# Replanning the takes of a graph-attention, mixing and FP4 feed-forward layer, with seven base chunks ahead of its tail

## The chip, the cores and the metric

One core of a Trainium2 chip runs the whole layer as one program with five instruction streams: TensorE (PE), VectorE (DVE), ScalarE (ACT), GpSimd (POOL) and SyncE (SP). The metric is the time of one execution on the device in microseconds, the median of several.

## The reference

`x` is 1250 x 1024 in float32, with 40000 edges `src -> dst`, sorted by `dst`.

```python
xn = layernorm(x)
x = x + gnn(xn, src, dst) + mix(xn)
x = x + ffn(layernorm(x))

gnn: h = rms_norm(xn) * rms_w @ W_down            # 1024 -> 256
     xl, xr = h @ Wl, h @ Wr                      # 4 heads of 64
     e = sum(leaky_relu(xl[src] + xr[dst]) * att) # per edge and head, self loops added
     out = softmax over the edges of each dst, weighting xl[src];  out @ W_up
mix: q, k, v = xn @ W.T + b;  (q @ k.T * SCALE) @ v @ Wo.T + bo   # no softmax
ffn: gate, up = fp4(y) @ fp4(gate_w).T, fp4(y) @ fp4(up_w).T
     fp4(silu(gate) * up) @ fp4(down_w).T         # blocks of 16 with e4m3 scales
```

## The kernel before, in words

The 1250 rows are ten chunks of 128 (the last has 98). Since the mixing has no softmax, it is computed as a chain of 1024 x 1024 products: the Gram matrix of the normalized rows, then `p`, `kv`, `t1`, `t2` (16 groups each, a group being one 128 x 512 result of eight accumulated products), at whose end one matrix stands in `big_a`; `base` is `xhat` times that matrix, two groups for each chunk, plus bias and x.

**Start.** SP loads x chunk by chunk (L442), between chunks 1 and 2 also the RMS weights as a column (L445) and `w_down` (L446). VectorE normalizes (L1308 to L1316), TensorE transposes (`turn_rows`, L805), ScalarE scales `w_down` by the RMS weights (`scale_wd`, L1106).

**Rounds.** The edges of the graph are worked in 62 rounds of up to six neighbours for each of 128 nodes. In each, POOL gathers rows (L564) and rescales (L686), VectorE forms scores (L1532, L1701, L1703, L1708) and sums (L1540), ScalarE takes exponentials (L1167) and multiplies (L1177). Meanwhile TensorE works through the groups `p` to `base` (L782) in four PSUM banks of `acc`: group n may begin once group n-4 has been taken. A take is one instruction, on VectorE for `p`, `kv`, `p0c` and `bias` (L1492, L1495, L1489, L1500), on ScalarE for `t1`, `t2` and `base` (L1090, L1096, L1093). Both engines run a fixed order, so a small planner (the loop that fills `round_of`, constants `PRODUCTS_AT`, `ROUND_0_AT`, `GROUP_STEP`, `SLOT_STEP`, `ROUND_OVER`, `TAKE_STEP`) gives every take the round at whose begin it stands. A take too late holds TensorE up, one too early the engine that takes.

**Tail.** The first `EARLY` chunks have their base before the tail. x is added to these by an accumulating transfer of POOL (`add_x`, L699), the bias too (`add_bias`, L708). For the later chunks SP loads x (L533) and the base products are made in the tail, inside `x2` (L939), with the two products of the graph part (L942). `X2_PLAN` gives for each (chunk, half) the bank, when TensorE makes it and when VectorE adds it to the residual (L1658). In iteration k of the tail TensorE transposes the quantized chunk k+1 (`turn_q`, L961), then the hidden chunk k-2 (L983), makes its x2, the down product of k-2 (L996) and gate and up of k+1 (`gate_up`, L972), which are sixteen products with one signal at their end. ScalarE normalizes chunk k+2 (L1058, L1059), copies the transposes (L1208, L1235), computes `silu` (L1243) and scales the down product (L1200), in this fixed order. VectorE's step k finds block maxima (L1300), scales and rounds chunk k+1 together with hidden chunk k-1 (L1632 to L1646), after the product silu * up (L1612).

Of the kernel before, what the change touches and what calls it, by code (L numbers as in the profile page):

```python
# [9 lines left out]
F32 = mybir.dt.float32  # L10
# [18 lines left out]
EARLY = 6  # L29
# [29 lines left out]
PRODUCTS_AT, GROUP_STEP = 168, {"p0c": 2.0, "bias": 1.0}  # L59
ROUND_0_AT, SLOT_STEP, ROUND_OVER, TAKE_STEP = 158, 0.95, 2.2, 0.7  # L60
# [3 lines left out]
BIAS_SUMS_AT, AHEAD = 43, 2  # L64
# [55 lines left out]
def gps_layer(nc, x, src, dst, rms_w, w_down, wl, wr, att, w_up, wq, bq, wk_t, bk, wv_t, bv,  # L120
# [9 lines left out]
    with ExitStack() as ctx:  # L130
# [72 lines left out]
        rms_col = sb("rms_col", [P, KB])  # L203
        s_in_bc = sb("s_in_bc", [P, 2])
# [26 lines left out]
        wd_in, rms_in, wlr_in = sem("wd_in"), sem("rms_in"), sem("wlr_in")  # L231
        edges_in = sem("edges_in")
# [56 lines left out]
        gu_full, silu_done, hid_done = sem("gu_full"), sem("silu_done"), sem("hid_done")  # L289
# [89 lines left out]
        off_ps = tpb[0:DG_HI, 1, 2 * DG_LO:2 * DG_LO + 2].bitcast(F32)  # L379
        lin_ps = tpb[0:NC, 0, 0:4 * H * C].bitcast(F32).rearrange("p (c h) -> p c h", c=C)  # L380
# [56 lines left out]
        def _(sp):  # L437
            for c in range(C):
# [4 lines left out]
                if c == 1:  # L443
                    with nc.allow_non_contiguous_dma(reason="columns of small vectors"):
                        sp.dma_start(rms_col[:], rms_w.rearrange("(k p) -> p k", p=P)).then_inc(rms_in, 16)  # L445
                    sp.dma_start(wd_sb, w_down.rearrange("(k p) d -> p k d", p=P)).then_inc(wd_in, 16)  # L446
# [317 lines left out]
        def _(pe):  # L764
# [46 lines left out]
            for c in range(2):  # L811
                turn_rows(c)
# [151 lines left out]
            def gate_up(c):  # L964
# [9 lines left out]
                mm.then_inc(gu_full, 1)  # L974
# [29 lines left out]
            for k in range(-1, C + 2):  # L1004
# [6 lines left out]
                if k == 2:  # L1011
                    turn_hidden(0)
                if 0 <= k - 2 < C:
                    down(k - 2)
                if 0 <= k + 1 < C:
# [8 lines left out]
        for g, (_, _, slots, _, _) in enumerate(ROUNDS):  # L1024
            while n < len(groups):
                kind, i, engine = groups[n]
                full = max(at, freed.get(n - 4, 0)) + GROUP_STEP.get(kind, 7.0)
                if full > begun:
# [3 lines left out]
                freed[n] = begun + 0.8  # L1032
# [12 lines left out]
        def _(act):  # L1045
# [63 lines left out]
            act.wait_ge(rms_in, 16)  # L1109
            act.wait_ge(wd_in, 16)  # L1110
            for k in range(3):
                scale_wd(k)
            take_rows(1)
            for k in range(3, KB):
# [110 lines left out]
            for k in range(-1, C + 2):  # L1225
# [13 lines left out]
                if 0 <= c < C:  # L1239
                    act.wait_ge(gu_full, c + 1)  # L1240
# [7 lines left out]
        def _(dve):  # L1248
# [353 lines left out]
            def tail_scales(k):  # L1602
# [6 lines left out]
                if k - 1 >= 0:  # L1609
                    c = k - 1  # L1610
                    dve.wait_ge(silu_done, c + 1)
# [153 lines left out]
```

## Time and profile before

| | us |
|---|---|
| median of 3 executions | 902.01 (901.41 to 905.28) |
| the profiled execution, own time | 905.27 |
| its span, first to last instruction | 903.4 |
| TensorE busy / VectorE busy | 855.8 / 794.7 |
| ScalarE busy / POOL busy | 563.1 / 497.2 |

The profiled execution's time is 1.9 us longer than its span. Matmul records are pipelined, and a 128x512 product in float32 has two records. The granted clock is TensorE's, as a share of 2.4 GHz, 0.50 being 1.2 GHz.

### The profile page before, as it was taken

The numbers are of one execution on the slowest core, as the hardware profiler recorded it, in microseconds if no ns is written. First come the engines' busy times: TensorE is split into PE (matmuls) and PEld (weight loads), VectorE is DVE, ScalarE is ACT, GpSimd is POOL, SyncE is SP. The second block draws the span as 40 slices with busy tenths as digits, with TensorE's granted clock in tenths as the row PEclk, the third lists the DMA queues.
The fourth block names the chain that finished last, engine by engine and source line by source line (L and its number), as shares of the span: only waits on it lengthen the run. The fifth ranks groups of instructions, "written<-read, shape, count | busy, mean of one in ns | idle before, by whom it ended". The sixth has DMA issues, their size and how long they took to land.

```text
span 903.4 us, 9499 instructions
## 1 busy us (share of the span) xinstructions
PE 855.8 (95%) x2744; PEld 421.2 (47%) x2754; DVE 794.7 (88%) x903; ACT 563.1 (62%) x1977; POOL 497.2 (55%) x527
## 2 busy tenths in 40 slices
PE   6899999999999999999999999999699999999855
PEld 5786455644444444444444444444244444444322
DVE  6999989689999999999999999999993078788994
ACT  3317532387658778779898988789894243243432
POOL 3405588667667677777777878877751130010001
PEclk7989999999999999999999999999699999999878
DMA  9331773735354433554336634338936563222335
GB/s 300 112 124 25 230 200 102 246 89 88 73 177 148 122 88 102 192 186 120 100 99 195 195 97 103 90 92 193 265 84 134 116 155 93 79 43 46 47 47 88
DMA packets 66578, 114.83 MB, mean 127 GB/s; under 512 B 29575, under 2 KB 36516, under 8 KB 66506
## 3 DMA queue, kind: packets, MB, share of 16 engines
q0 software_dynamic: 22144, 63.68, 30.2%
q1 hardware_dynamic: 44378, 50.51, 17.4%
q8 instruction: 22, 0.36, 0.2%
q14 instruction: 34, 0.28, 0.1%
HBM read 89.28 MB, written 17.17 MB: 118 GB/s over the span
## 4 chain that ended last, share of the span: by engine, by line
DVE 59%; PE 32%; issue 4%; ACT 3%; DMA 1%; SPq 0%; ACTq 0%; POOL 0%; DVEq 0%
PE acc L782 21%; DVE acc_sb L1540 11%; DVE z L1703 10%; DVE turned L1532 10%; DVE turned L1701 10%; PE acc L939 2%; PE acc L972 2%; PE turned L939 2%; PE acc L942 2%; PE turned L996 1%; ACT round_mem L1177 1%; DVE z L1708 1%; DVE big_b L1492 1%; DMA big_b<-in_x 1%; DVE big_a L1495 1%
## 5 line engine op out<-in xcount | busy, mean ns | idle before, releaser
L564 POOL DMA_INDIRECT round_mem<-msg_table,idx x352 | 349.5, 993 | 103.0 <-issue 82.6
L1177 ACT ACTIVATE round_mem<-round_mem,pz 128x65 f32<-128x65 f32 x1408 | 354.0, 398 | 6.8 <-DVE acc_sb L1540 2.8
L782 PE MATMUL acc<-wslot,big_a 128*128 128x512 f32 x512 | 220.3, 593 | 0.0
L782 PEld LDWEIGHTS acc<-wslot,big_a 128*128 128x128 f32 x512 | 97.3, 190 | 121.3 <-issue 121.1
L1540 DVE TENSOR_REDUCE acc_sb<-round_mem 128x260 f32<-128x1820 f32 (+1 forms) x62 | 121.6, 1962 | 14.1 <-ACT round_mem L1177 12.0
L782 PE MATMUL acc<-big_b,wslot 128*128 128x512 f32 x256 | 110.0, 593 | 0.0
L782 PE MATMUL acc<-wslot,big_b 128*128 128x512 f32 x256 | 110.0, 593 | 0.0
L1532 DVE TENSOR_TENSOR turned<-round_mem,turned 128x1560 f32<-128x1560 f32 (+1 forms) x62 | 105.4, 1700 | 2.3 <-DMA round_mem<-msg_table,idx 0.2
L1703 DVE TENSOR_REDUCE z<-turned 128x24 f32<-128x1560 f32 (+1 forms) x62 | 105.1, 1696 | 2.1
L1167 ACT ACTIVATE pz<-z 128x7 f32<-128x7 f32 (+1 forms) x248 | 55.4, 295 | 78.9 <-DVE z L1708 77.9
L1701 DVE SCALAR_TENSOR_TENSOR turned<-turned,att_sb 128x1536 f32<-128x1536 f32 (+1 forms) x62 | 103.6, 1671 | 0.1
L782 PE MATMUL acc<-big_a,xhat_t 128*128 128x512 f32 x192 | 85.6, 609 | 6.0 <-ACT big_b L1093 6.0
L782 PE MATMUL acc<-big_b 128*128 128x512 f32 (+3 forms) x240 | 78.7, 487 | 0.0
L782 PEld LDWEIGHTS acc<-big_b,wslot 128*128 128x128 f32 x256 | 48.7, 190 | 61.1 <-issue 60.6
L782 PEld LDWEIGHTS acc<-wslot,big_b 128*128 128x128 f32 x256 | 48.7, 190 | 61.1 <-issue 61.1
L782 PEld LDWEIGHTS acc<-big_a,xhat_t 128*128 128x128 f32 x192 | 37.5, 196 | 54.6 <-issue 46.6
L686 POOL TENSOR_TENSOR round_mem<-acc_sb,pz 128x260 f32<-128x260 f32 x62 | 44.1, 711 | 33.1 <-DVE acc_sb L1540 28.1
L782 PEld LDWEIGHTS acc<-big_b 128*128 128x128 f32 x240 | 42.3, 191 | 34.0 <-issue 28.4
L1243 ACT ACTIVATE round_mem<-acc,cscale 128x512 f32<-128x512 f32 x10 | 6.9, 687 | 73.8 <-PE acc L972 61.7
L735 POOL TENSOR_TENSOR rstd<-small,minus_half 128x1 f32<-128x1 f32 x10 | 6.3, 626 | 81.8 <-ACT small L1190 81.8
L741 POOL DMA_DIRECT2D out_x<-acc_sb x9 | 7.9, 878 | 74.8 <-ACT acc_sb L1200 74.8
L782 PE MATMUL acc<-xhat_t,big_a 128*128 128x256 f32 x160 | 40.6, 414 | 3.1 <-ACT xhat_t L1101 3.1
(231 smaller groups left out, 1009.8 us busy)
## 6 DMA issues: line engine op xcount, KB each, us to landing
big_b<-in_x SPq DMA_DIRECT2D x12, 512.0 KB, 9.8
round_mem<-msg_table,idx POOLq DMA_INDIRECT x352, 2.8
big_b<-big_b POOLq DMA_DIRECT2D x9, 512.0 KB, 5.9
out_x<-big_b SPq DMA_DIRECT2D x9, 512.0 KB, 3.1
out_x<-acc_sb POOLq DMA_DIRECT2D x9, 512.0 KB, 5.6
wslot<-in_wv_t SPq DMA_DIRECT2D x2, 2048.0 KB, 9.9
wslot<-in_wk_t SPq DMA_DIRECT2D x2, 2048.0 KB, 9.4
wslot<-in_wo_t SPq DMA_DIRECT2D x2, 2048.0 KB, 9.6
```

Source lines behind the costliest of these rows:

```text
L564: pool.indirect_dma_start(xg[g % 4][:, j, :], None, msg_table, bass.IndirectOffsetOnAxis(idx[:, c, j0 + j:j0 + j + 1], 0)).then_inc(xg_in[ ...
L686: nc.gpsimd.tensor_tensor(halves_of[g % 3][:, :, :, n].rearrange("p i (h d) -> p i h d", d=MR), running[c].rearrange("p (i h d) -> p i h d ...
L782: mm = nc.tensor.matmul(o(acc[:, n % 4, :]), a, b, start=first, stop=last)
L939: nc.tensor.matmul(to, xhat_t[:, k, c * NC:(c + 1) * NC], mat_a[:, k, h * HALF:(h + 1) * HALF], start=(k == 0), stop=False)
L942: mm = nc.tensor.matmul(to, gnn_tr[:, k, c * NC:(c + 1) * NC], wup_sb[:, k, h * HALF:(h + 1) * HALF], start=(c < EARLY and k == 0), stop=( ...
L972: mm = nc.tensor.matmul(acc[0:NC, 2 + h, :], q_t[c % 2][:, k, 0:NC], wgu_sb[:, k, h * HALF:(h + 1) * HALF], start=(k == 0), stop=(k == KB ...
L1167: ins = nc.scalar.activation(pz[:, g % 2, 0:slots + 1, h], z[:, g % 3, 0:slots + 1, h], ACT.Exp, scale=-1.0, bias=z[:, (g + 1) % 3, top_sl ...
L1177: ins = nc.scalar.activation(to[:, :, j], xg[g % 4][:, j, h * HR + 1:(h + 1) * HR], ACT.Copy, scale=pz[:, g % 2, j, h:h + 1])
L1532: return nc.vector.tensor_tensor(m4[:, 0:n], xg[g % 4][:, 0:n, :].rearrange("p j (h d) -> p j h d", d=HR)[:, :, :, 0:MR], receiver.unsquee ...
L1540: nc.vector.tensor_reduce(running[c].rearrange("p (i f) -> p i f", i=2), halves_of[g % 3][:, :, :, 0:n + 1], AX.X, ALU.add).then_inc(sum_d ...
L1701: step(nc.vector.scalar_tensor_tensor(m4[:, 0:slots, :, 1:MR], m4[:, 0:slots, :, 1:MR], 0.0, att_sb[0:NC].unsqueeze(1).to_broadcast([NC, s ...
L1703: step(nc.vector.tensor_reduce(zz[:, 0:slots, :], m4[:, 0:slots], AX.X, ALU.add))
```

## The change

Four edits in one:

1. The planner's constants and rules are replaced, so most takes move one or two rounds up. The sums for the bias start a round earlier (`BIAS_SUMS_AT` 43 to 42).
2. `EARLY` is 7: chunk 6's two base groups come before the tail. In `X2_PLAN` (7, 1) takes the place and bank of (6, 1).
3. The RMS weights are loaded as eight rows of 128, transposed by TensorE and copied to the column by ScalarE.
4. `gate_up` signals after the gate half too; silu waits for this alone and VectorE for both. For the last chunk gate and up are put ahead of a down product.

```diff
-EARLY = 6
+EARLY = 7
-PRODUCTS_AT, GROUP_STEP = 168, {"p0c": 2.0, "bias": 1.0}
-ROUND_0_AT, SLOT_STEP, ROUND_OVER, TAKE_STEP = 158, 0.95, 2.2, 0.7
+PRODUCTS_AT, GROUP_STEP = 173.5, {"p0c": 2.0, "bias": 1.0}
+ROUND_0_AT, SLOT_STEP, ROUND_OVER, TAKE_STEP = 166.5, 0.95, 2.2, 0.7
...
-BIAS_SUMS_AT, AHEAD = 43, 2
+BIAS_SUMS_AT, AHEAD = 42, 2
...
-    (5, 1, 2, (-2, 7), (0, 0)), (2, 1, 0, (-2, 7), (-1, 2)), (6, 1, 6, (-2, 7), (0, 2)), (2, 0, 5, (-2, 9), (-1, 2)),
+    (5, 1, 2, (-2, 7), (0, 0)), (2, 1, 0, (-2, 7), (-1, 2)), (7, 1, 6, (-2, 7), (0, 2)), (2, 0, 5, (-2, 9), (-1, 2)),
...
-    (7, 1, 4, (0, 0), (3, 0)), (6, 0, 1, (0, 1), (2, 0)), (7, 0, 6, (1, 0), (3, 0)), (5, 0, 0, (1, 0), (2, 2)),
+    (6, 1, 4, (0, 0), (2, 0)), (6, 0, 1, (0, 1), (2, 0)), (7, 0, 6, (1, 0), (3, 0)), (5, 0, 0, (1, 0), (2, 2)),
...
-                    with nc.allow_non_contiguous_dma(reason="columns of small vectors"):
-                        sp.dma_start(rms_col[:], rms_w.rearrange("(k p) -> p k", p=P)).then_inc(rms_in, 16)
+                    sp.dma_start(rms_rows[:], rms_w.rearrange("(k p) -> k p", p=P)).then_inc(rms_in, 16)
...
-            for c in range(2):
-                turn_rows(c)
+            turn_rows(0)
+            pe.wait_ge(rms_in, 16)
+            nc.tensor.transpose(rms_ps, rms_rows[:], ident[0:KB, 0:KB]).then_inc(rms_tp, 1)
+            turn_rows(1)
...
-                mm.then_inc(gu_full, 1)
+                    mm.then_inc(gate_full if h == 0 else gu_full, 1)
...
+                if k + 1 == C - 1:
+                    gate_up(k + 1)
                 if 0 <= k - 2 < C:
                     down(k - 2)
-                if 0 <= k + 1 < C:
+                if 0 <= k + 1 < C - 1:
                     gate_up(k + 1)
...
-                full = max(at, freed.get(n - 4, 0)) + GROUP_STEP.get(kind, 7.0)
-                if full > begun:
+                full = max(at, freed.get(n - 4, 0)) + GROUP_STEP.get(kind, 6.93)
+                if full > begun + (2.5 if engine == "act" else 0.0):
                     break
                 round_of[n], at = g, full
                 begun += TAKE_STEP if engine == "dve" else 0.0
-                freed[n] = begun + 0.8
+                freed[n] = begun + (0.8 if engine == "dve" else 3.6)
...
             take_rows(0)
-            act.wait_ge(rms_in, 16)
+            act.wait_ge(rms_tp, 1)
+            nc.scalar.copy(rms_col[:], rms_ps).then_inc(rms_taken, 1)
+            act.wait_ge(rms_taken, 1)
             act.wait_ge(wd_in, 16)
-            for k in range(3):
+            for k in range(2):
                 scale_wd(k)
             take_rows(1)
-            for k in range(3, KB):
+            for k in range(2, KB):
                 scale_wd(k)
...
-                    act.wait_ge(gu_full, c + 1)
+                    act.wait_ge(gate_full, c + 1)
...
                     dve.wait_ge(silu_done, c + 1)
+                    dve.wait_ge(gu_full, c + 1)
```

The order on ScalarE at the end of the rounds, before (an `ACTIVATE big_a<-acc` is a take of `t2`, a `COPY big_b<-acc` one of `base`, `pz<-z` and `round_mem<-round_mem,pz` the exponentials and multiplications of a round):

```order
L1096 ACTIVATE big_a<-acc 128x512
L1167 ACTIVATE pz<-z 128x7 x4
L1177 ACTIVATE round_mem<-round_mem,pz 128x65 x24
L1096 ACTIVATE big_a<-acc 128x512
L1167 ACTIVATE pz<-z 128x6 x4
L1177 ACTIVATE round_mem<-round_mem,pz 128x65 x20
L1096 ACTIVATE big_a<-acc 128x512
L1167 ACTIVATE pz<-z 128x7 x4
L1177 ACTIVATE round_mem<-round_mem,pz 128x65 x24
L1093 COPY big_b<-acc 128x512
```

and after, over the same rounds:

```order
L1102 ACTIVATE big_a<-acc 128x512
L1175 ACTIVATE pz<-z 128x7 x4
L1185 ACTIVATE round_mem<-round_mem,pz 128x65 x24
L1099 COPY big_b<-acc 128x512
L1175 ACTIVATE pz<-z 128x6 x4
L1185 ACTIVATE round_mem<-round_mem,pz 128x65 x20
L1099 COPY big_b<-acc 128x512
L1175 ACTIVATE pz<-z 128x7 x4
L1185 ACTIVATE round_mem<-round_mem,pz 128x65 x24
L1099 COPY big_b<-acc 128x512
```

These are rounds 53, 54, 55 and the begin of 56. Where the last three takes of `t2` stood, now the last of `t2` and the first two of `base` stand, and the third of `base` has the first one's place.

The order on TensorE in iteration 0 of the tail, before (`L961` the transposes of chunk 1, `L939` base products, `L942` those of the graph part, `L972` gate and up):

```order
L961 MATMUL turned<-identb,round_mem 128x128 x8
L939 MATMUL turned<-big_a,xhat_t 128x512 x8
L942 MATMUL turned<-wslot,xr_sb 128x512 x2
L972 MATMUL acc<-wslot,round_mem 128x512 x16
L939 MATMUL acc<-big_a,xhat_t 128x512 x8
L942 MATMUL acc<-wslot,xr_sb 128x512 x2
L961 MATMUL turned<-identb,round_mem 128x128 x8
```

and after:

```order
L965 MATMUL turned<-identb,round_mem 128x128 x8
L946 MATMUL turned<-wslot,xr_sb 128x512 x2
L976 MATMUL acc<-wslot,round_mem 128x512 x16
L946 MATMUL acc<-wslot,xr_sb 128x512 x2
L965 MATMUL turned<-identb,round_mem 128x128 x8
```

The sixteen base products between the two transposes are gone; those of (7, 1) stand where (6, 1) stood, and chunk 6's stand ahead of the tail.

On POOL, in the tail's first iterations, the change (`L701` and `L737` are `add_x` and the root of the deviation, `L710` is `add_bias`):

```order
L737 TENSOR_TENSOR rstd<-small,minus_half 128x1
L701 DMA big_b<-in_x 128x1024
L710 DMA big_b<-big_b 128x1024 x3
L737 TENSOR_TENSOR rstd<-small,minus_half 128x1 x2
L701 DMA big_b<-in_x 98x1024
```

The first transfer of x (chunk 6) is new here; the three biases behind it are those of chunks 4, 8 and 6, before 4, 8 and 7.

## Rows read from the trace of the kernel before

**Rows 1.** The page: busy time of the engines, and the chain's shares.

```profile
PE 855.8 (95%) x2744; PEld 421.2 (47%) x2754; DVE 794.7 (88%) x903; ACT 563.1 (62%) x1977; POOL 497.2 (55%) x527
...
DVE 59%; PE 32%; issue 4%; ACT 3%; DMA 1%; SPq 0%; ACTq 0%; POOL 0%; DVEq 0%
```

**Rows 2.** Timeline of PE: start, us, engine, line, instruction, idle before.

```profile
175.40 15.19 PE L782 MATMUL acc<-wslot,big_a 128*128 128x512 f32 x35
...
630.39 1.02 PE L782 MATMUL acc<-big_b,minus_half 128*128 128x512 f32 x2
634.62 2.06 PE L782 MATMUL acc<-big_b,minus_half 128*128 128x512 f32 x2 [3.22 <-ACT big_a L1096]
642.70 19.77 PE L782 MATMUL acc<-big_a,xhat_t 128*128 128x512 f32 x39 [6.01 <-ACT big_b L1093]
```

**Rows 3.** Timeline of ACT, takes.

```profile
618.91 0.58 ACT L1096 ACTIVATE big_a<-acc 128x512 f32<-128x512 f32 x1
...
641.97 0.58 ACT L1093 COPY big_b<-acc 128x512 f32<-128x512 f32 x1
...
714.43 0.58 ACT L1093 COPY big_b<-acc 128x512 f32<-128x512 f32 x1 [6.28 <-PE acc L782]
```

**Rows 4.** Busy time by stretch: length, PE, PEld, DVE, ACT, POOL, clock, DMA.

```profile
642.70:648.57 5.87, 5.87 (x8) 2.49 (x9) 5.65 (x6) 5.57 (x23) 4.54 (x6) 0.52 1.03 394
851.67:859.45 7.78, 7.69 (x23) 2.82 (x24) 7.33 (x14) 1.88 (x6) 0.56 (x1) 0.69 0.24 46
```

**Rows 5.** Timeline of DVE, begin of round 2.

```profile
185.74 1.76 DVE L1701 SCALAR_TENSOR_TENSOR turned<-turned,att_sb 128x1536 f32<-128x1536 f32 x1
```

**Rows 6.** Timeline of DVE, statistics of the third chunk.

```profile
13.43 0.69 DVE L1313 BATCH_NORM_STATS2 stats<-big_b 128x6 f32<-128x512 f32 x1 [3.91 <-DMA big_b<-in_x]
```

**Rows 7.** Transfers of 0 to 16 us: GB/s by 0.4 us, one issue's landing.

```profile
GB/s 0 0 0 0 113 174 317 389 440 348 430 358 61 76 50 206 315 305 330 289 266 302 371 425 405 443 394 443 399 420 430 399 440 410 420 420 420 420 399 420
...
rms_col<-in_rms_w SPq DMA_DIRECT2D x1, 4.0 KB, 7.4
```

**Rows 8.** Chain of waits, where TensorE takes over: start, us.

```profile
45.14 2.85 PE turned L790 x80
```

**Rows 9.** Busy time by TensorE iteration of the tail (columns as rows 4).

```profile
749.80:771.74 21.94, 21.29 (x64) 9.63 (x65) 15.88 (x30) 5.16 (x9) 0.56 (x1) 1.00 0.21 66
771.74:785.99 14.25, 14.20 (x48) 6.52 (x48) 13.43 (x22) 2.94 (x6) 1.49 (x2) 1.00 0.18 28
785.99:801.33 15.34, 14.61 (x56) 6.78 (x57) 14.72 (x27) 7.45 (x15) 1.73 (x2) 1.00 0.26 103
...
832.15:848.16 16.01, 14.81 (x56) 6.73 (x57) 13.53 (x23) 7.51 (x13) 1.43 (x2) 1.00 0.23 34
```

**Rows 10.** Timeline of DVE in the tail; L1300 begins a step.

```profile
764.66 1.03 DVE L1646 TENSOR_TENSOR round_mem<-round_mem 128x1024 bf16<-128x1024 bf16 x2
...
771.94 0.69 DVE L1658 SCALAR_TENSOR_TENSOR big_b<-acc,big_b 128x512 f32<-128x512 f32 x1 [5.64 <-PE acc L942]
...
773.34 1.75 DVE L1300 TENSOR_REDUCE round_mem<-round_mem 128x96 f32<-128x1536 f32 x1
...
804.78 1.75 DVE L1300 TENSOR_REDUCE round_mem<-round_mem 128x96 f32<-128x1536 f32 x1 [1.78 <-ACT round_mem L1059]
...
850.33 1.75 DVE L1300 TENSOR_REDUCE round_mem<-round_mem 128x96 f32<-128x1536 f32 x1 [0.62 <-ACT round_mem L1059]
...
863.87 1.75 DVE L1300 TENSOR_REDUCE round_mem<-round_mem 128x96 f32<-128x1536 f32 x1
```

**Rows 11.** The page: group of silu.

```profile
L1243 ACT ACTIVATE round_mem<-acc,cscale 128x512 f32<-128x512 f32 x10 | 6.9, 687 | 73.8 <-PE acc L972 61.7
```

**Rows 12.** Timelines of PE, ACT, DVE around the last silu.

```profile
879.02 3.19 PE L996 MATMUL turned<-wslot,round_mem 128*128 128x512 bf16 x7 [1.68 <-ACT round_mem L1235]
...
887.16 1.11 ACT L1200 ACTIVATE acc_sb<-turned,cscale 128x1024 f32<-128x1024 f32 x1
...
887.29 0.75 DVE L1612 SCALAR_TENSOR_TENSOR round_mem<-acc,cscale,round_mem 128x512 f32<-128x512 f32 x1 [3.35 <-ACT round_mem L1243]
```

More of the change, by code:

```diff
@@ L203, in gps_layer @@
         rms_col = sb("rms_col", [P, KB])
+        rms_rows = sb("rms_rows", [KB, P])
         s_in_bc = sb("s_in_bc", [P, 2])
@@ L231, in gps_layer @@
         wd_in, rms_in, wlr_in = sem("wd_in"), sem("rms_in"), sem("wlr_in")
+        rms_tp, rms_taken = sem("rms_tp"), sem("rms_taken")
         edges_in = sem("edges_in")
@@ L288, in gps_layer @@
         q_done, q_tp, q_taken = sem("q_done"), sem("q_tp"), sem("q_taken")
-        gu_full, silu_done, hid_done = sem("gu_full"), sem("silu_done"), sem("hid_done")
+        gate_full, gu_full, silu_done, hid_done = sem("gate_full"), sem("gu_full"), sem("silu_done"), sem("hid_done")
         h_done, h_tp, h_taken = sem("h_done"), sem("h_tp"), sem("h_taken")
@@ L379, in gps_layer @@
         off_ps = tpb[0:DG_HI, 1, 2 * DG_LO:2 * DG_LO + 2].bitcast(F32)
+        rms_ps = tpb[:, 0, 0:2 * KB].bitcast(F32)
         lin_ps = tpb[0:NC, 0, 0:4 * H * C].bitcast(F32).rearrange("p (c h) -> p c h", c=C)
```

## The prediction

> **What bounds the kernel now.** I read the page first: TensorE is busy for 95% of the span and VectorE for 88%, yet the chain that ended last runs 59% through VectorE and 32% through TensorE [rows 1]. Two engines are full side by side, so I went to the timeline of each and asked at every stretch which one the other waits for.
>
> Three facts come out of it.
>
> First, TensorE works without a gap from 175.40 us, where the "p" products begin, up to 630.39 [rows 2]. That is 66 groups (16 each of p, kv, t1 and t2, two of base) and one tiny one, so a group of eight 128x512 products takes (630.39 - 175.40) / 66 = 6.89 us. Then it stands still twice: 3.22 us before the second bias product, until ScalarE has taken t2's last group, and 6.01 us before the third base group, until ScalarE has taken the first base group at 641.97 [rows 2, 3]. These groups were full long before (t2's last at 175.4 + 64 x 6.89 + 0.5 = 616.9, the first base group at 623.8). They waited for their place in the table of takes, and a bank is refilled only when the take four groups back is done. After the second stall the granted clock is 0.52, the lower of the two levels (1.2 of 2.4 GHz), for 5.87 us in which eight matmul records run instead of some fourteen: 2.9 us more lost [rows 4]. VectorE's rounds end long before TensorE's last base group (taken at 714.43 [rows 3]) and the tail cannot start earlier. So TensorE's stream sets the time from the start of the products to the start of the tail.
>
> Second, ahead of that: VectorE stands 3.91 us until the third chunk of x lands at 13.4 [rows 6], from there works through, and hands to TensorE at 45.14 [rows 8], from where the chain is TensorE's. What chunk 2 gains, all gains.
>
> Third, the tail. Each TensorE iteration begins with the transposes of a quantized chunk. From 785.99 to 848.16 four of them take 15.5 us each and hold 14.6 to 14.8 us of TensorE work [rows 9]: nearly TensorE's pace, plus a wait. VectorE's own step is 13.5 us (850.33 to 863.87 [rows 10]). After 850 VectorE sets the pace.
>
> **The change, part by part.**
>
> *Takes replanned.* I moved every take to its new round and set full times at 6.89 us a group against the rounds' begins. The first p group, full at 182.3, is taken at the begin of round 2, at 185.7 with its own 0.7 us added [rows 5]: no wait. At the end t2's last group (full 616.9) takes ScalarE's slot at 618.91, and each base group a slot two places earlier than now; the slot of 641.97, which held the first base group, holds the third (full 639.7) [rows 3]. No group is taken before it is full, and no bank is asked for before its take. Both stalls go, and with them the clock's fall: 3.22 + 6.01 + 2.9 = **-12.1 us**. What is late next is TensorE itself.
>
> *Seven chunks ahead.* Two more base groups, 2 x 6.89 = **+13.8 us** before the tail.
>
> *RMS weights as rows.* The column load is 4 KB, 7.4 us to landing. While its 4-byte pieces run, four slices of 0.4 us carry 61, 76, 50 and 206 GB/s where the slices around reach 350 to 440 [rows 7]: 1.6 us that do 0.4 us of work, so 1.2 us lost ahead of w_down and chunk 2. Eight rows of 512 B cost next to nothing of that. The bounds are 0 (chunk 2 late for another reason) and 3.91, all of VectorE's wait; I take the slices' value, **-1.2 us**. The added transpose and the small copy lie before ScalarE's wait for w_down and are hidden by it; without that cover they would cost two small operations, under 0.5 us. By the Trainium skill, DMA: Bandwidth & Descriptors, section "Measured (HBM→SBUF, 128 partitions, SWDGE, issued from GpSimd)", a packet costs about 10.5 ns and 64 of them on an engine 0.67 us; as an estimate the term would be -0.7 and the sum half a microsecond worse.
>
> Start of the tail: 13.8 - 12.1 - 1.2 = **+0.5 us**.
>
> *The tail without chunk 6.* TensorE's iteration 0 (749.80 to 771.74) is 21.3 us of work, 13.8 of it the base products of two halves: (7, 1), which moves up into the place of (6, 1), and (6, 0), whose base is now done before the tail; both are gone from here [rows 9]. VectorE waits 5.64 us for just these, before 771.94 [rows 10]. In the new order VectorE has both residuals of chunk 6 at once, so its step 2 starts at 766.3 + 2 x 0.6 + 0.8 = 768.3 in place of 773.34. TensorE is done with iteration 0 at 771.74 - 13.8 = 757.9 and has nothing until the next chunk is quantized at 765.4 (the first half of the pair at 764.66 [rows 10]): **a new gap of some 7.5 us**. After the stall of 6.01 us and after a gap of 2.7 us before 851.67 the clock stood at 0.52 and 0.69 [rows 4]; so I expect it to fall here, for 2.8 us of lost work. Iteration 1 then runs 765.4 + 14.2 + 2.8 = 782.4 (before 785.99). The Trainium skill, TensorE: Matmul & The Clock Gate, section "What's actually happening", says the lower rate is the default and only activity lifts it, so idling is paid again on return; that speaks against this edit and agrees with rows 4. Were it not so here, the first rival below holds.
>
> *silu on the gate product alone.* Silu and the normalization queued behind it on ScalarE start one half, 1.7 us, earlier. That is the 1.78 us VectorE waits for the normalization before 804.78 [rows 10], in two steps of four, and smaller ones. So iterations close up to TensorE's own work: 15.3 for iteration 2 (its wait for the first hidden transposes stays), then 14.7 three times: 782.4, 797.7, 812.4, 827.1, 841.8, before 848.16. VectorE's step 7 begins 1.8 us after gate and scale are through, at 843.6, before 850.33: **-6.7 us**. From there both kernels run at 13.5 us a step.
>
> *Last gate and up ahead of a down product.* The last silu now waits for nothing but the gate. VectorE's wait of 3.35 us at 887.29 shrinks to 0.7, but that is not the end's chain: ScalarE's scaling of down product 6, which follows silu (0.69 us [rows 11]) at 887.16 [rows 12], starts the alternation of down, scale, copy that ends the kernel. It moves only to the end of the down product, some 886.1, as the same TensorE work lies ahead of it: **-1.0 us** (bounds 0, and -3.8 if the half clock of 879.02 [rows 12] and its 2.8 us weren't met).
>
> *Chunk 6's x* is now added by a POOL transfer put ahead of the bias of chunk 4, for which VectorE doesn't wait now. Bounds 0 and +1.2, half a megabyte at the 420 GB/s of rows 7; I take 0, since no wait for a bias shows in the tail.
>
> **Sum:** +0.5 - 6.7 - 1.0 = **-7.2 us**. The profiled execution's own time is 905.27 (span 903.4), which would become 898.1. It is 3.3 us above the median 902.01; on the median the same step gives **894.8 us**.
>
> **Rivals.**
>
> *The clock holds in the new gap.* For it: it was 1.00 across iteration 0 [rows 9], with short gaps only. Against: rows 4. Then iteration 2 starts when VectorE's step 2 delivers, 768.3 + 12.45 = 780.75 (a step's first result comes 12.45 us after its begin, as from 773.34 to 785.8), and all later ones 1.6 us earlier: 893.2. Chance 0.15.
>
> *The stalls were dearer in this execution than in the median one.* The 3.3 us between them are about one fall of the clock. If the median execution had the stalls but not the fall, 2.9 us of my gain aren't there: 897.7. Chance 0.2.
>
> *The plan misses, and TensorE still stalls (slower).* If ScalarE, whose multiplications fill most of each round, comes to the moved takes after its multiplications and thus as late as now, the 12.1 us stay while 13.8 us were added: 902.01 + 4.9 = 906.9. It decides from 7.2 us of remaining stall on; below that the tail still pays. Against it: the new slots are ScalarE's own take slots of now, filled one group further on. Chance 0.06.
>
> *The RMS edit does nothing* (chunk 2 lands as before): 896.0. Within the range; part of the forecast's 0.59.
>
> **How the numbers follow.** Likeliest 894.8, chance 0.59. Range: below, the clock holding (893.2) with 2 us more of chunk 2's wait, 891.2; above, the second rival with the RMS term at nothing, 898.9. This leaves out the slower case and a little of each end. A measurement here can tell 0.5%, 4.5 us, so the border is 897.5: faster 0.80 (0.55 of the forecast's 0.59, the first rival, half of the second), same 0.16 (the rest of both and the slower case where it falls just inside), slower 0.04.
>
> **What would show it.** TensorE's products without a wait from about 174 until about 715, clock 1.00 throughout; the third chunk's statistics near 12.2; a TensorE gap of 7 to 8 us near 758 with a lower clock behind it; no VectorE wait for the normalization in steps 3 to 7; iterations of 14.7 us. A stall of several microseconds among the base groups, or VectorE waiting for a product at a take, would prove the plan wrong; a tail that keeps 15.5 us per iteration would prove the silu term wrong.

## The result, and the profile after

| | before | changed |
|---|---|---|
| median, this comparison | 903.49 us (901.41 to 905.28, 4 runs) | 894.26 us (893.55 to 895.54, 4 runs) |
| ratio, 95% interval | | 0.990 (0.987 to 0.993) |
| median, a later comparison | 904.07 us (11 runs) | 894.04 us (4 runs), ratio 0.989 (0.987 to 0.990) |
| profiled execution, own time; span | 905.27; 903.4 | 895.54; 893.7 |
| TensorE busy / VectorE busy | 855.8 / 794.7 | 853.9 / 794.1 |

The kernel is 9 to 10 us faster, and my 894.8 lies 0.5 to 0.8 us from the measured medians. How much of that is merit is the question of the last sections, since the step itself was forecast at -7.2 us and measured at -9.2 to -10.0.

The page of the changed kernel, the chain's shares (before: [rows 1]):

```profile
PE 853.9 (96%) x2755; PEld 422.0 (47%) x2755; DVE 794.1 (89%) x903; ACT 564.4 (63%) x1980; POOL 495.6 (55%) x528
...
PE 84%; DVE 7%; issue 5%; DMA 2%; ACT 1%; POOL 0%; SPq 0%; ACTq 0%; DVEq 0%; POOLq 0%
```

TensorE has 84% of the chain, after 32%. It is not busier. Before, the chain left TensorE at the second stall and went back through VectorE's rounds to their begin; now there is no stall through which it could leave.

TensorE's timeline around the place of the stalls (start, us, engine, line, instruction, idle before), to be held against [rows 2]:

```profile
603.44 11.32 PE L784 MATMUL acc<-big_b,wslot 128*128 128x512 f32 x26
614.60 13.90 PE L784 MATMUL acc<-big_a,xhat_t 128*128 128x512 f32 x32
628.33 1.88 PE L784 MATMUL acc<-big_b,minus_half 128*128 128x512 f32 x4
630.04 82.14 PE L784 MATMUL acc<-big_a,xhat_t 128*128 128x512 f32 x191
```

No idle time stands behind any row: from 604 to 712 TensorE is busy for all 108.0 us at clock 1.00. The twelve remaining base groups take 82.4 us, 6.87 each, and the tail's first transposes start at 712.45. Before, they started at 714.23, with two groups fewer ahead of them.

ScalarE's last take of `t2` and its first three of base groups (compare [rows 3]) show by how much they moved:

```profile
616.03 0.58 ACT L1102 ACTIVATE big_a<-acc 128x512 f32<-128x512 f32 x1
...
625.26 0.58 ACT L1099 COPY big_b<-acc 128x512 f32<-128x512 f32 x1
...
631.47 0.58 ACT L1099 COPY big_b<-acc 128x512 f32<-128x512 f32 x1
...
639.44 0.58 ACT L1099 COPY big_b<-acc 128x512 f32<-128x512 f32 x1
```

The first base group was taken at 641.97 and is now taken at 625.26.

The tail, TensorE's iterations (length, then busy time of PE, PEld, DVE, ACT, POOL, clock, DMA; before: [rows 9]):

```profile
748.02:763.62 15.60, 7.93 (x33) 3.38 (x33) 14.98 (x28) 5.16 (x9) 0.56 (x1) 0.85 0.40 96
763.62:780.53 16.91, 16.91 (x48) 7.81 (x49) 16.29 (x31) 4.44 (x9) 1.49 (x2) 0.84 0.23 56
780.53:795.87 15.34, 14.66 (x57) 6.79 (x56) 12.99 (x22) 7.26 (x15) 1.18 (x2) 1.00 0.26 103
795.87:810.36 14.49, 14.49 (x57) 6.71 (x56) 12.71 (x20) 6.65 (x12) 1.57 (x2) 1.00 0.24 38
825.15:839.88 14.73, 14.70 (x58) 6.83 (x57) 13.89 (x24) 6.44 (x12) 1.43 (x2) 1.00 0.24 37
```

Read the first two together. Iteration 0 shrank from 21.94 to 15.60 us but holds only 7.93 us of work. Iteration 1 has the same 48 matmul records as before and takes 16.91 in place of 14.25, because its clock is 0.84. TensorE's timeline shows the new gap and what follows it:

```profile
763.62 1.03 PE L965 MATMUL turned<-identb,round_mem 128*128 128x128 bf16 x8 [7.08 <-DVE round_mem L1655]
764.44 9.37 PE L943 MATMUL turned<-big_a,xhat_t 128*128 128x512 f32 x16
...
780.98 7.09 PE L943 MATMUL acc<-big_a,xhat_t 128*128 128x512 f32 x16
```

Sixteen base records take 9.37 us right after the gap and 7.09 one iteration later. The iterations from 795.87 to 839.88 are TensorE's own work without a wait; behind them it waits again in each.

VectorE's timeline, the begins of its steps 2 to 4 and 7, and of its last instruction (before: [rows 10]):

```profile
766.42 1.75 DVE L1308 TENSOR_REDUCE round_mem<-round_mem 128x96 f32<-128x1536 f32 x1
781.60 1.75 DVE L1308 TENSOR_REDUCE round_mem<-round_mem 128x96 f32<-128x1536 f32 x1
797.82 1.75 DVE L1308 TENSOR_REDUCE round_mem<-round_mem 128x96 f32<-128x1536 f32 x1 [0.91 <-ACT round_mem L1065]
...
841.60 1.75 DVE L1308 TENSOR_REDUCE round_mem<-round_mem 128x96 f32<-128x1536 f32 x1 [0.61 <-ACT round_mem L1065]
...
888.33 1.28 DVE L1672 SCALAR_TENSOR_TENSOR big_b<-turned,cscale,big_b 128x1024 f32<-128x1024 f32 x1 [5.87 <-PE turned L1000]
```

Step 7 begins 8.73 us earlier than the 850.33 of before.

The end has something new. ScalarE's last scaled down products, by its timeline (before: [rows 12]):

```profile
875.83 1.11 ACT L1208 ACTIVATE acc_sb<-turned,cscale 128x1024 f32<-128x1024 f32 x1 [2.77 <-PE turned L1000]
...
879.41 1.11 ACT L1208 ACTIVATE acc_sb<-turned,cscale 128x1024 f32<-128x1024 f32 x1 [1.99 <-PE turned L1000]
...
884.75 1.11 ACT L1208 ACTIVATE acc_sb<-turned,cscale 128x1024 f32<-128x1024 f32 x1 [3.74 <-DMA out_x<-acc_sb]
```

The first two stand 3.58 us apart, so the third was due at 882.99. It came 1.76 us later, because its buffer was still being read by the accumulating transfer to `out` of two chunks before. That delay reaches the end of the kernel.

### The profile page after: what moved, and what is told of

The parts are those of the page before. It is cut to its first block, busy times and chain, and to the rows that moved or that the text cites. A ratio compares the mean times of both kernels' runs of the same rounds, so it can differ in the third digit from the quotient of the medians.

```text
span 893.7 us, 9524 instructions
## 1 busy us (share of the span) xinstructions
PE 853.9 (96%) x2755; PEld 422.0 (47%) x2755; DVE 794.1 (89%) x903; ACT 564.4 (63%) x1980; POOL 495.6 (55%) x528
## 3 DMA queue, kind: packets, MB, share of 16 engines
q1 hardware_dynamic: 43210, 49.98, 17.4%
## 4 chain that ended last, share of the span: by engine, by line
PE 84%; DVE 7%; issue 5%; DMA 2%; ACT 1%; POOL 0%; SPq 0%; ACTq 0%; DVEq 0%; POOLq 0%
PE acc L784 73%; PE acc L943 2%; PE turned L943 2%; PE acc L946 2%; DMA big_b<-in_x 1%; PE acc L976 1%; DMA out_x<-acc_sb 1%; PE turned L946 1%; PE turned L792 1%; PE turned L1000 1%; DVE big_b L1316 1%; DVE stats L1321 1%; DVE stats L1322 1%; DVE round_mem L1641 1%; DVE round_mem L1308 1%
## 5 line engine op out<-in xcount | busy, mean ns | idle before, releaser
L784 PE MATMUL acc<-big_a,xhat_t 128*128 128x512 f32 x224 | 96.5, 592 | 0.0
L784 PEld LDWEIGHTS acc<-big_a,xhat_t 128*128 128x128 f32 x224 | 42.6, 190 | 53.5 <-issue 53.5
L737 POOL TENSOR_TENSOR rstd<-small,minus_half 128x1 f32<-128x1 f32 x10 | 5.9, 586 | 89.6 <-ACT small L1198 89.6
L1093 ACT COPY big_a<-acc 128x512 f32<-128x512 f32 x16 | 9.0, 587 | 54.5 <-PE acc L784 35.7
```

Of the source, the lines that this page charges most:

```text
L784: mm = nc.tensor.matmul(o(acc[:, n % 4, :]), a, b, start=first, stop=last)
L1093: nc.scalar.copy(mat_a[:, m, h * HALF:(h + 1) * HALF], a).then_inc(t, 1)
```

## The experiments

Two theories stood against each other at the outset. Mine was a sum of nearly independent terms. The rival was that the seventh chunk is what pays, the replanned takes only making room for it. The sum itself says otherwise: two base groups cost 13.8 us ahead of the tail and return less than that. Undoing one edit at a time tells them apart. Each kernel is the changed one but for its edit; ratios are to the kernel before, timed beside each group of experiments: its median was 903.36 beside the first four, 903.60 beside the next four, 904.07 beside the three after them and 903.25 beside the last.

**RMS weights as a column again.**

```diff
-sp.dma_start(rms_rows[:], rms_w.rearrange("(k p) -> k p", p=P))
+sp.dma_start(rms_col[:], rms_w.rearrange("(k p) -> p k", p=P))
...
-nc.tensor.transpose(rms_ps, rms_rows[:], ident[0:KB, 0:KB])
...
-nc.scalar.copy(rms_col[:], rms_ps)
```

> The changed kernel, but the RMS weights come as a column of 4-byte pieces again. Theory (the column delays the third chunk of x and everything behind it): its statistics begin near 13.4 in place of 11.48, the products near 175.4 in place of 173.34, and the whole ends 2.1 us later, 896.3. My prediction's size of this term was 1.2 (895.5). Rival (the early gain is lost again somewhere behind, since the takes were planned for the new begins): within 0.3 of 894.3.

Measured: 895.3 us (894.83 to 896.77), ratio 0.990 (0.987 to 0.993). That is 1.0 to 1.3 us above the changed kernel (894.26 and 894.04), and the executions' ranges overlap. But the profile denies the reading of [rows 6]: VectorE's timeline of this kernel has, with the column in place,

```profile
11.34 0.69 DVE L1318 BATCH_NORM_STATS2 stats<-big_b 128x6 f32<-128x512 f32 x1 [1.70 <-DMA big_b<-in_x]
```

which is no later than with rows (11.48 in the changed kernel). One execution is no measure of this landing, so the suspected cost was tripled below.

The reading of [rows 7] has its answer in a trace too. The same slices of 0.4 us in the changed kernel, with rows in place of the column:

```profile
GB/s 0 0 0 0 102 205 317 338 358 430 379 424 168 184 228 300 292 276 259 338 384 405 438 389 443 420 399 461 379 451 379 461 369 451 379 461 369 451 389 420
```

The dip of slices 13 to 16 is still there: 168, 184, 228 and 300 GB/s for 61, 76, 50 and 206 of before. Against 420 GB/s that is 0.8 us lost with rows and 1.2 with the column. Over all profiles it is 0.7 to 1.1 us in the eleven with rows and 1.2 in the two with the column. So the column explains at most half a microsecond of the dip, and my term had charged it with the whole.

**Six base chunks, everything else kept.**

```diff
-EARLY = 7
+EARLY = 6
...
-(7, 1, 6, (-2, 7), (0, 2))
+(6, 1, 6, (-2, 7), (0, 2))
...
-(6, 1, 4, (0, 0), (2, 0))
+(7, 1, 4, (0, 0), (3, 0))
```

> The changed kernel with six base chunks ahead of the tail and the old X2_PLAN; the replanned takes, the rows and the gate signal stay. Theory by my own accounts: without two base groups the tail's first transposes begin 13.8 us earlier, at 698.7 in place of 712.45; the tail then costs TensorE 14.1 more, but 7 to 8 of that fill the new gap and its lower clock, so the end comes 6 us earlier: 888.3. Rival: the seventh chunk was needed, because the attention result or the transfers of x and bias are not there by 698.7 (attention lands at 698.5, the x transfers begin there), and the tail starts or stumbles later: 892 to 902, same or slower than the changed kernel.

Measured: **885.9 us** (884.62 to 887.1), ratio 0.980 (0.977 to 0.982). The seventh chunk costs 8.3 us; without it the other edits take 17.5 us off the kernel. That is 2.4 us better than my theory had, and the rival, that the attention result or the transfers would not be there, is refuted. TensorE's timeline of this kernel at the begin of the tail and at the chunk's base products:

```profile
699.71 0.60 PE L956 MATMUL turned<-ident,acc_sb 128*128 128x128 f32 x4
...
748.64 7.03 PE L943 MATMUL acc<-big_a,xhat_t 128*128 128x512 f32 x16
755.51 1.88 PE L946 MATMUL acc<-wslot,xr_sb 128*128 128x512 f32 x4
757.23 0.61 PE L965 MATMUL turned<-identb,round_mem 128*128 128x128 bf16 x8
```

There is no gap ahead of chunk 2's transposes, and its step 7 on VectorE:

```profile
832.57 1.75 DVE L1308 TENSOR_REDUCE round_mem<-round_mem 128x96 f32<-128x1536 f32 x1 [0.62 <-ACT round_mem L1065]
```

The tail begins 12.7 us earlier than in the changed kernel and step 7 begins 9.0 us earlier, though this execution's products began 1.0 us later (174.34 for 173.34). So of the 13.8 us that the two groups cost, the tail gives back 3.7. In the changed kernel the work taken out of iteration 0 leaves TensorE idle for 7.08 us and then slow by 2.3 us, together 9.4 of the 13.8.

**The old planner.** The constants of before, `full > begun`, and `freed[n] = begun + 0.8`.

> The changed kernel with the old planner's constants and rules and the old place of the bias sums. Theory: the two stalls are back (3.22 + 6.01, and 2.9 to 4.2 of lower clock around them), so 906.4 to 907.7, slower than the kernel before. Rival: with the rows loaded earlier or with fourteen base groups the old table does less harm, 900 or less.

Measured: 906.63 us (905.74 to 910.28, 12 runs), ratio 1.004 (1.003 to 1.006). Both stalls are back, by TensorE's timeline:

```profile
631.63 2.08 PE L784 MATMUL acc<-big_b,minus_half 128*128 128x512 f32 x2 [3.20 <-ACT big_a L1102]
639.76 85.31 PE L784 MATMUL acc<-big_a,xhat_t 128*128 128x512 f32 x192 [6.06 <-ACT big_b L1099]
724.91 0.60 PE L956 MATMUL turned<-ident,acc_sb 128*128 128x128 f32 x4
```

The twelve groups take 85.3 us in place of 82.4, at a clock of 0.54 for the first 5.87 us. The replanned takes are worth 12.4 to 12.6 us.

**silu waits for gate and up both.**

```diff
-act.wait_ge(gate_full, c + 1)
+act.wait_ge(gu_full, c + 1)
```

> The changed kernel, but silu waits for gate and up both, as before. Theory: VectorE waits again for the normalization by 1 to 1.8 us in every second step and TensorE's iterations stretch from 14.5 to 15.3: four of them, +3 us, and the last silu 1.7 us later: 897 to 899. Rival: the tail is TensorE's anyway and only the last step shows it: 895 to 896.

Measured: 896.72 us (895.76 to 899.29), ratio 0.993 (0.990 to 0.995), so 2.6 us, just under the 897 to 899 that I expected. The waits of before return on VectorE's timeline, at steps 4 and 6:

```profile
797.91 1.75 DVE L1308 TENSOR_REDUCE round_mem<-round_mem 128x96 f32<-128x1536 f32 x1 [1.78 <-ACT round_mem L1065]
812.67 1.75 DVE L1308 TENSOR_REDUCE round_mem<-round_mem 128x96 f32<-128x1536 f32 x1
828.73 1.75 DVE L1308 TENSOR_REDUCE round_mem<-round_mem 128x96 f32<-128x1536 f32 x1 [1.78 <-ACT round_mem L1065]
```

Now that the seventh chunk turned out a loss, the next question was whether its gap could be filled, and what the lower clock behind it is worth.

**(7, 0) moved into the gap.**

```diff
-(7, 0, 6, (1, 0), (3, 0))
+(7, 0, 6, (0, 1), (3, 0))
```

> The changed kernel with seven chunks, but x2 of (7, 0), base products and all, is made one place earlier, at (0, 1) ahead of chunk 2's transposes, in the gap of 7.08 us. Theory (the loss of the seventh chunk is that gap and its lower clock alone): the gap is gone, TensorE's iteration 1 ends near 771 in place of 780.5, VectorE's step 7 begins near 833 to 834 in place of 841.60, and the time is that of six chunks, 886 to 887. Rival (VectorE is the bound from step 2 on, or chunk 2's transposes are late by the 1.7 us that the product overruns the gap): 890 to 893.

Measured: 895.12 us (894.58 to 897.49), ratio 0.991 (0.990 to 0.993). My theory (886 to 887) fell, and the rival's 890 to 893 was missed as well: the move gains nothing. TensorE's timeline:

```profile
764.16 0.61 PE L965 MATMUL turned<-identb,round_mem 128*128 128x128 bf16 x8
...
778.32 1.03 PE L965 MATMUL turned<-identb,round_mem 128*128 128x128 bf16 x8 [8.32 <-DVE round_mem L1655]
779.14 8.17 PE L943 MATMUL acc<-big_a,xhat_t 128*128 128x512 f32 x16
```

The gap is not filled but handed on: iteration 1 ends at once and TensorE waits 8.32 us for chunk 3, which VectorE has quantized no earlier (its steps begin at 750.30, 765.65 and 780.51, without a pause). The next base products, those of (8, 1), still stand behind chunk 3's transposes and take 8.17 us, at a granted clock of 0.83. In this program TensorE can't begin an iteration before VectorE has quantized its chunk. So I take it that work moved up by one place helps only if all later x2 steps move up too; with seven chunks this was not run.

**The gap filled with work for nothing.** 32 bfloat16 products whose result nobody reads.

```diff
+if k == 0:
+    pe.wait_ge(x2_taken, user_of(5))
+    for i in range(32):
+        nc.tensor.matmul(turned[0:NC, HALF:2 * HALF], identb[0:NC, 0:NC], wgu_sb[:, i % KB, 0:HALF], start=True, stop=True)
```

> The changed kernel with 32 products of 128x128 by 128x512 in bfloat16 in the gap of 7.08 us, whose result nobody reads; they only keep TensorE busy. Theory (the idle time lets the clock fall, which costs 2.2 us after it): base products of (7, 0) take 7.1 us in place of 9.37, the clock of that stretch is 1.00, the gap itself stays as idle time filled, and the time falls by 2 us to 892. Rival (VectorE's step sets the pace there, so a faster iteration 1 gives nothing): 894.3 with the clock at 1.00.

Measured: 893.82 us (893.23 to 894.22), ratio 0.989 (0.987 to 0.990). TensorE's timeline:

```profile
756.72 7.07 PE L1028 MATMUL turned<-wslot,identb 128*128 128x512 bf16 x32
763.98 0.62 PE L965 MATMUL turned<-identb,round_mem 128*128 128x128 bf16 x8 [0.19 <-DVE round_mem L1659]
764.44 7.08 PE L943 MATMUL turned<-big_a,xhat_t 128*128 128x512 f32 x16
```

Kept busy, the engine keeps its clock, 1.00 across the stretch: 7.08 in place of 9.37 us. From step 1 of VectorE (751.44) to its step 7 (840.56) this kernel takes 89.12 us, the changed one 90.50 (751.10 to 841.60). So the trace shows 1.4 us gained there, and the medians, 0.2 to 0.4 us apart, don't resolve it. The gap's clock is a small part of the chunk's loss.

**Buffers of their own for the last two scaled products, six chunks.**

```diff
+y_late = [wslot[0][0:NC, 4 * I + i * D:4 * I + (i + 1) * D] for i in range(2)]
...
-if c >= 2:
+if 2 <= c < 7:
     act.wait_ge(added[c % 2], 16 * (c // 2))
```

> Six chunks as in a2_six_chunks, and the last two scaled down products get buffers of their own, in the room of the W_up weights, which no product reads by then; so they wait for no accumulating transfer. Theory (the wait of 3.74 us for out_x in the changed kernel's last scaling is met by some executions only): the median falls by 0.3 to 1, to 885 to 885.6, and no execution waits there. Rival (buffers were free in most executions): 885.9, no difference.

Measured: 885.5 us (884.3 to 886.45), ratio 0.980 (0.978 to 0.981), against 885.9 for six chunks alone: no difference that can be told. The wait for `out_x` shows in three of nine profiles with seven chunks (3.74, 2.30 and 2.23 us), not in that of six, so it has little weight in a median.

**The x2 steps with base products spread over iterations 0 to 6**, one each, with those buffers. ScalarE's normalization of chunk 9 moves behind its deviation, since its last residual now comes later.

```diff
+(6, 0, 1, (0, 1), (2, 0)), (7, 1, 4, (1, 0), (3, 0)), (5, 0, 0, (1, 0), (2, 2)), (7, 0, 1, (2, 0), (3, 1)),
+(8, 1, 0, (3, 0), (5, 0)), (8, 0, 1, (4, 0), (5, 1)), (9, 1, 0, (5, 0), (6, 1)), (9, 0, 1, (6, 0), (7, 1)),
```

> As b4_six_and_buffers, with the seven x2 steps that hold base products spread one to an iteration, 0 to 6, in place of two in iteration 0 and none in iteration 6 ((9, 0) is made at (6, 0) and added at (7, 1), chunk 9 is normalized behind its deviation). Theory (TensorE sets the pace of iterations 1 to 5, VectorE from step 7 on, so work moved from iteration 0 to 6 lets VectorE begin step 7 near 826 in place of 832.6): VectorE then waits some 5 us for chunk 9's normalization ahead of step 8, and 2 to 3 us remain: 883. Rival (the longer chain through chunk 9 costs more than that): 886 to 889.

Measured: 886.37 us (884.84 to 886.92), ratio 0.980 (0.979 to 0.982): no gain. Half of the mechanism is there, by VectorE's timeline:

```profile
825.93 1.75 DVE L1311 TENSOR_REDUCE round_mem<-round_mem 128x96 f32<-128x1536 f32 x1 [0.38 <-ACT round_mem L1066]
845.21 1.75 DVE L1311 TENSOR_REDUCE round_mem<-round_mem 128x96 f32<-128x1536 f32 x1 [5.20 <-ACT round_mem L1066]
```

Step 7 begins 6.0 us earlier than with the buffers alone (831.89), and step 8 then waits 5.20 us for chunk 9's normalization and begins only 0.2 us earlier (845.21 for 845.40). I had expected 2 to 3 us to remain of the gain and had left out that the steps get no shorter: step 7, with its own residual behind it, takes 14.1 us up to this wait in place of 13.5. TensorE meanwhile stands idle for 11.64 us ahead of chunk 9's transposes.

**Three columns ahead of the third chunk.** The RMS column and both bias columns.

> The changed kernel with three columns of 4-byte pieces ahead of W_down and the third chunk: the RMS weights as before, and the two bias columns that otherwise load after the edges. The third chunk's statistics began at 10.66 to 11.80 in four executions with rows and at 11.34 and 13.43 in two with one column. Theory (each column costs the 1.2 us of my prediction): they begin near 15, the products near 177, and the whole takes 3.6 us more than the changed kernel, 898. Rival (a column costs at most half a microsecond and the rest is how the transfers happen to fall): they begin at 11 to 13, and the time is 894.5 to 896.

Measured: 895.83 us (894.79 to 899.28), ratio 0.991 (0.990 to 0.993), 1.8 us above the changed kernel timed beside it (894.04), with ranges that overlap. The third chunk's statistics, by VectorE's timeline:

```profile
12.56 0.69 DVE L1317 BATCH_NORM_STATS2 stats<-big_b 128x6 f32<-128x512 f32 x1 [2.91 <-DMA big_b<-in_x]
```

The theory of 1.2 us a column falls. Eleven profiled executions with rows have this begin at 10.66 to 11.99, one column has 13.43 and 11.34, three have 12.56. A column costs half a microsecond or so (1.8 / 3 = 0.6), and a single execution varies by more.

**Gate and up of the last chunk behind the down product again.** The two lines that put `gate_up` ahead are taken out.

> The changed kernel, but gate and up of the last chunk come behind the down product again. Theory (the last hidden chunk is on the end's chain, and so is the alternation of down, scale and copy, within 0.5 us of each other): the last silu comes 1.7 us later, the first scaling behind it 1 us earlier, and the end 0.7 us later: 895. Rival (the order is worth the whole 1.7 us or more): 896 or more.

Measured: 895.09 us (894.34 to 895.54), ratio 0.990 (0.988 to 0.992), 1.05 us above the changed kernel timed beside it. In size as expected, but the ranges overlap.

**The changed kernel again.**

> The changed kernel itself once more, beside the other runs of this call. Expected: 894.3 as before; the third chunk's statistics begin between 10.6 and 11.8, the products between 172.3 and 174.4. It tells how much of a difference of one microsecond is the execution's own.

Measured: 894.04 us (893.15 to 896.09), ratio 0.989 (0.987 to 0.990). Statistics at 11.37, products at 173.66.

**Five base chunks.** `EARLY = 5`; chunk 5's x comes by the load of the later chunks.

> As a2_six_chunks with five base chunks ahead of the tail in place of six: chunk 5's base products are made in the tail, its x is loaded and not added by a transfer. Theory (before the attention result lands, near 696, TensorE has nothing else to do, so the base groups that fill the time until then are free, and only those behind it cost): TensorE stands still some 10 us from 686 on, the tail begins near 696 in place of 699.71 and holds 14 us more of TensorE's work, so 895, 9 to 10 us slower than six; that is, six is the best count, with seven too many by 8. Rival (base products in the tail hide beside VectorE's steps whatever their number, as most of chunk 6's did): 882 to 886.

Measured: 903.26 us (902.17 to 905.63, 11 runs), ratio 1.000 (0.999 to 1.001). Slower than six by 17.4, by more than I had worked out. TensorE's timeline:

```profile
694.29 1.12 PE L956 MATMUL turned<-ident,acc_sb 128*128 128x128 f32 x4 [9.63 <-DMA acc_sb<-gnn_dram]
695.53 3.75 PE L946 MATMUL turned<-wslot,xr_sb 128*128 128x512 f32 x4
699.07 2.38 PE L946 MATMUL acc<-wslot,xr_sb 128*128 128x512 f32 x4
...
745.40 10.03 PE L943 MATMUL turned<-big_a,xhat_t 128*128 128x512 f32 x16 [5.77 <-DVE big_b L1667]
```

and VectorE's, at the residual that TensorE waited for:

```profile
744.04 0.69 DVE L1667 SCALAR_TENSOR_TENSOR big_b<-turned,big_b 128x512 f32<-128x512 f32 x1 [5.08 <-DMA big_b<-big_b]
```

The attention result bounds the begin of the tail, as expected. What I had missed shows in the last row of TensorE's and in VectorE's: in iteration 0 a residual waited 5.08 us for a bias transfer, TensorE waited for that residual, and the base products behind it took 10.03 us at a granted clock of 0.70.

From the tail's begin to step 7 this kernel takes 157.0 us (694.29 to 851.25) and the one with six chunks 132.9 (699.71 to 832.57). The 24.1 us between them are two more base groups (14.1), the longer wait of TensorE for a residual (5.77 for 0.60, so 5.2), the slower base products behind it (10.03 for 7.13, so 2.9), and the slower first products after the 9.63 us of standing still (3.75 and 2.38 for 1.95 and 1.88, so 2.3). The bias transfer is thus behind some 8 of the 17.4 us. As an estimate from these rows, five chunks without it would be 9 us slower than six, which is what my theory had.

So of the three counts six is the best. With five, TensorE waits for the attention result. With seven, it comes to the tail at 712.45, 14 us past the time at which POOL, which waits for the whole result, goes on (698.48), and works there on something that the tail would have hidden in part beside VectorE. With six it comes at 699.71, where POOL goes on at 699.42. TensorE's own first need is the result's first part only, the rows of two chunks, which arrives earlier: with five chunks TensorE goes on at 694.29 and POOL at 697.42. By this lead of 3.1 us, as an estimate, even six chunks pass TensorE's landing by some 3 us.

## Why the prediction was right, and where its sum was off

The prediction's -6.7 us for the tail splits into -3.6 for the begin of iteration 2 (chunk 6 gone) and -3.1 for the iterations behind it (silu). The terms, with what undoing each one cost in the medians, against the middle of the changed kernel's 894.04 and 894.26:

| term | predicted | measured |
|---|---|---|
| takes replanned | -12.1 | -12.5 |
| RMS weights as rows | -1.2 | -1.1, not resolved |
| seventh chunk, net | +10.2 (13.8 - 3.6) | +8.3 |
| silu on gate alone | -3.1 | -2.6 |
| last gate and up first | -1.0 | -0.9, not resolved |
| sum | -7.2 | -8.8; directly -9.2 to -10.0 |

- **The stalls** were read rightly: late takes, not late products, and a clock that falls with them. In the profiles they are worth 13.4 us (products' begin to tail's begin is 539.1 us in the changed kernel and 552.5 with the old planner), because the bias products behind the first stall ran slowly too (2.06 us for two records, [rows 2]). My 12.1 left these out.
- **The new gap** was put at 7.5 us and is 7.08; its lower clock at 2.8 us and is 2.3; iteration 1 at 17.0 and is 16.9. The first rival, that the clock would hold, was wrong. Made to hold by filler work, it moves VectorE's step 7 by 1.4 us where the rival had 1.6. The Trainium skill's rule, TensorE: Matmul & The Clock Gate, section "What's actually happening", that only activity lifts the rate, agrees with the pair of 9.37 us after idling and 7.08 us after filler.
- **The closing up of the iterations** came as written: 15.3, 14.5, 14.8, 14.7 where 15.3 and three times 14.7 stood. VectorE's wait before step 4 is 0.91 us, not gone.
- **The third rival** (the plan misses) did not come about, and the kernel with the old planner shows what it would have cost: 906.6, where the rival had 906.9. That the two agree is partly luck, as the step is +3.3 us from the 903.36 timed beside it, where the rival had +4.9 from 902.01.
- **The RMS term** fits in size, which no run resolves, and was wrong in its proof. The rows it rested on, [rows 6, 7], show one execution in which the third chunk landed late, and a dip of the transfers of which the larger part, 0.8 of 1.2 us, is there without the column; in the profiled pair it made 2.06 us (products at 173.34 for 175.40), of which the column explains a quarter (0.5) to a half (1.1). Three columns in place of rows made 1.8 us, one made 1.1. From the packet cost in the Trainium skill, DMA: Bandwidth & Descriptors, section "Measured (HBM→SBUF, 128 partitions, SWDGE, issued from GpSimd)", the prediction had an estimate of 0.7 us a column; the 0.6 us a column with three agrees with it better than with my 1.2, and the 1.1 with one column, not resolved, doesn't choose.
- **What was not foreseen** is the wait for the accumulating transfer in the last scaling, 1.76 us in the profiled execution. I had followed the alternation of down, scale and copy without the buffer behind it. Against step 7 the scaling of down product 6 comes 2.6 us earlier in that execution (875.83 for 887.16, step 7 at 841.60 for 850.33), not the 1.0 of the prediction, and the transfer takes 1.76 of it back. In the repeated run of the changed kernel it comes 0.9 us earlier (878.12, step 7 at 842.15), without such a wait. So the -1.0 fits, and a single profile can't show it.

**What is off is the sum and its base, and that the two misses cancel is luck.** The prediction took -7.2 us from 902.01, the median of three executions. The change measured 2 to 3 us more than this, and the kernel before measured 903.25 to 904.07 in the later comparisons, 1.2 to 2.1 us more. Where the profiled pair, whose span falls by 9.7 us, has the difference:

| stage | before | after | step | predicted |
|---|---|---|---|---|
| to the products' begin | 175.40 | 173.34 | -2.06 | -1.2 |
| products to the tail's begin | 538.83 | 539.11 | +0.28 | +1.7 (13.8 - 12.1) |
| the tail's begin to step 7 | 136.10 | 129.15 | -6.95 | -6.7 |
| step 7 to the end | 53.07 | 52.10 | -0.97 | -1.0 |

So the missing 2.5 us are the stall term (1.4), an early landing that varies by as much (0.9) and little in the tail. The medians have it otherwise: there the stalls' undoing costs 0.4 us more than predicted, and the seventh chunk 1.9 less, while its net in the profiles is 13.8 - 3.7, as predicted. The changed kernel's two profiled executions, 895.54 and 896.09, are its slowest in either comparison, so part of this is how executions fall at either end. It stays open, as does the 0.4 to 1.2 us by which the direct measurement exceeds the terms' -8.8. The second rival, that the stalls' lower clock was missing from the median execution, is refuted by 12.5 us of undoing them.

The prediction had both halves of the largest finding in its sum, +13.8 and -3.6, and did not say what they mean: that one of the edits loses some 8 us and the change would be nearly twice as good without it.

## What to carry to other kernels

Put each edit of a combined change on its own line with its sign, and ask of every positive one why it is there: here the other edits gave 17.5 us and the seventh chunk took 8.3 back. Work that fills an engine while it waits for a result is worth having up to about the landing of that result. Beyond it the work costs its length, less what moving it saves behind: two groups of 13.8 us cost 8.3. Look for the landing in the trace to choose the amount, then run the counts beside it (five, six and seven chunks: 903.3, 885.9, 894.1 us). Moving one piece of work into a gap of one engine did not help here, because another engine gave the next signal: look for which one does.

## What the runs showed of the hardware

- The landing of the third chunk, an early transfer, varies by 1.3 us over eleven executions of kernels with the same begin (10.66 to 11.99 us), and the products begin at 172.3 to 174.3. The two go together only in part: with 11.26 in two executions the products begin at 172.54 and at 173.69. A term of 1 us in such a place can't be read from one profile.
- Where the lower clock falls at the end of the tail differs between executions of the same kernel. In the repeated run of the changed kernel down and gate-up behind 843 ran at a granted clock of 1.00, and TensorE then waited longer and ran the last gate and up at 0.56:

```profile
843.49 1.90 PE L1000 MATMUL turned<-wslot,round_mem 128*128 128x512 bf16 x8 [2.23 <-ACT round_mem L1243]
845.23 3.62 PE L976 MATMUL acc<-wslot,round_mem 128*128 128x512 bf16 x16
854.71 1.04 PE L965 MATMUL turned<-identb,round_mem 128*128 128x128 bf16 x8 [5.87 <-DVE round_mem L1655]
...
869.95 6.41 PE L976 MATMUL acc<-wslot,round_mem 128*128 128x512 bf16 x16 [0.74 <-ACT round_mem L1216]
```

In the first profile the same pieces took 2.48 and 4.77 us (granted clock 0.76), the wait was 4.16, and the last gate and up took 4.55 (0.78). From step 7 to VectorE's last instruction that is 45.0 us (without the transfer's delay) against 46.7, in one and the same program.
